# Extra matmuls beside the maxima where two attention units meet, the first unit's turn three items sooner, and GpSimd's padding after the first rows

## The reference

```python
def mla_attention(x, Wq, Wdkv, Wuk, Wuv, Wo, ln_g, ln_b):      # t = 2048 rows, 16 heads of 8
    q = (x @ Wq.T).reshape(b, t, N_HEADS, HEAD_DIM).transpose(0, 2, 1, 3)
    latent = layernorm(x @ Wdkv.T, ln_g, ln_b)
    k = (latent @ Wuk.T) ...; v = (latent @ Wuv.T) ...
    q, k = apply_rope(q), apply_rope(k)
    scores = jnp.einsum('bhqd,bhkd->bhqk', q, k) / np.sqrt(HEAD_DIM)
    scores = jnp.where(causal, scores, -jnp.inf)
    attn = jax.nn.softmax(scores, axis=-1)
    out = jnp.einsum('bhqk,bhkd->bhqd', attn, v)...
    return out @ Wo.T

x = x + mla_attention(rmsnorm(x, norm1_w), ...)
x = x + moe(rmsnorm(x, norm2_w), ...)
```

## Time and profile before

| | |
|---|---|
| three runs, us | 1656.7, 1664.8, 1669.15; median 1664.8 |
| the profiled execution | 1654.05 us, span of the core 1652.3 us |
| mean granted clock of PE | 0.864 |
| busy: PE, DVE, ACT, POOL | 1229.8, 1169.2, 953.3, 582.1 us (74, 71, 58, 35%) |

### The profile page before, as it was taken

One profiled execution on the slowest core, in us unless ns is written; L12 is line 12 of the kernel. 1 busy time (PEld: TensorE's weight loads), 2 busy tenths in 40 slices (PEclk: granted clock), 3 DMA queues, 4 the chain that ended last, 5 costly groups with the idle time before them and its releaser, 6 DMA issues. The chain is left out here.

```text
span 1652.3 us, 36830 instructions
## 1 busy us (share of the span) xinstructions
PE 1229.8 (74%) x14007; PEld 648.0 (39%) x14007; DVE 1169.2 (71%) x2634; ACT 953.3 (58%) x1539; POOL 582.1 (35%) x1039
## 2 busy tenths in 40 slices
PE   2755564466667778999998576776878899998848
PEld 2753454366442222223333265653222222233337
DVE  4348698735768889997775355576888999786235
ACT  2226775322345678888887442244666788878622
POOL 2430078146654331221111564575341111111236
PEclk9977676678569999999999788757999999999869
DMA  9252000021000000000010152000000000000023
GB/s 256 74 175 90 1 4 3 24 67 55 1 3 2 1 2 1 1 2 9 21 28 27 51 138 60 2 1 1 1 2 1 2 1 1 2 1 2 1 76 40
DMA packets 56799, 50.77 MB, mean 31 GB/s; under 512 B 7921, under 2 KB 52066, under 8 KB 56178
## 3 DMA queue, kind: packets, MB, share of 16 engines
q1 hardware_dynamic: 48818, 37.77, 8.2%
q0 software_dynamic: 6864, 9.55, 2.3%
q10 hardware_dynamic: 944, 1.10, 0.2%
HBM read 36.16 MB, written 21.35 MB: 35 GB/s over the span
## 5 line engine op out<-in xcount | busy, mean ns | idle before, releaser
L1902 DVE TENSOR_REDUCE arena<-psum 128x1 f32<-128x512 f32 (+4 forms) x1152 | 681.0, 654 | 141.6 <-PE psum L1708 96.9
L1843 ACT ACTIVATE arena<-psum 128x1024 f32<-128x1024 f32 (+3 forms) x640 | 557.9, 899 | 180.8 <-PE psum L1730 172.0
L1746 PE MATMUL psum<-arena 128*9 128x256 f32 (+2 forms) x4352 | 339.1, 388 | 0.8 <-POOL arena L1962 0.8
L1708 PE MATMUL psum<-arena 64*128 64x128 bf16 (+3 forms) x1664 | 224.9, 319 | 96.4 <-DVE arena L1902 86.1
L1730 PE MATMUL psum<-arena 64*128 64x512 bf16 (+3 forms) x1280 | 228.8, 357 | 22.8 <-ACT arena L1843 15.5
L1962 POOL TENSOR_SCALAR_AFFINE_SELECT arena<-arena 128x256 f32<-128x256 f32 x256 | 103.0, 406 | 369.0 <-ACT arena L1843 365.6
L1708 PEld LDWEIGHTS psum<-arena 64*128 64x128 bf16 x1664 | 69.9, 96 | 274.2 <-DVE arena L1902 233.4
L1730 PEld LDWEIGHTS psum<-arena 64*128 64x128 bf16 x1280 | 63.3, 94 | 175.6 <-ACT arena L1843 77.1
L1746 PEld LDWEIGHTS psum<-arena 128*9 128x9 f32 x4352 | 67.8, 89 | 152.5 <-issue 118.2
L1940 POOL CAST arena<-arena 128x16 bf16<-128x16 f32 x64 | 16.3, 255 | 284.3 <-DVE arena L1907 282.1
L698 ACT ACTIVATE small<-psum,YT 128x128 f32<-128x128 f32 x168 | 52.5, 364 | 93.4 <-PE psum L651 93.2
(11 more groups left out here) (368 smaller groups left out, 2015.1 us busy)
## 6 DMA issues: line engine op xcount, KB each, us to landing
regions<-sorted_rows SPq DMA_DIRECT2D x11, 741.8 KB, 14.1
big_w<-in_w SPq DMA_DIRECT2D x2, 2048.0 KB, 20.3
arena<-taps SPq DMA_DIRECT2D x16, 256.0 KB, 3.4
arena<-taps SPq DMA_DIRECT2D x4, 1024.0 KB, 10.8
ACCn<-regions SPq DMA_DIRECT2D x48, 64.5 KB, 1.8
ACCn<-made_rows SPq DMA_DIRECT2D x12, 256.0 KB, 3.8
w<-in_w SPq DMA_DIRECT2D x2, 1024.0 KB
sorted_rows<-arena SPq DMA_DIRECT2D x1, 1483.5 KB, 14.5
```

Source lines behind the costliest of these rows:

```text
L1708: mm = pe.matmul(psum[:, bank_of(("max", (v, m + r))), at:at + w], plain_q[v % 2][rows, a, i * P:(i + 1) * P], keys[rows, 2 * hq + a, key: ...
L1746: mm = pe.matmul(psum[32 * hh:32 * hh + 9, O_BANK, lo:hi], values[:, tile_of(v, j), 4 * hq + hh, :], prob[(t + hh // 2) % N_PROB][:, hh % ...
L1843: act.activation(prob[t % N_PROB][:, :, off:GW], both, ACT.Exp, scale=INV_SQRT_HD).then_inc(a_got, 1)
L1902: dve.tensor_reduce(place, rows, AX.X, ALU.max).then_inc(a_max_got, 1)
```

## The change

It has six edits. (1) `plan` starts the second pass of unit 0 six items after its last item and not nine. (2) The event "out" moves ahead, to just before an even place, so that it stands ahead of a pair of items, or a little more ahead than before. (3) `thin_pairs` collects the items that stand between the last `weigh` of one unit and the first of the next, and those ahead of the first `weigh` of all; ahead of each such pair PE issues one `keep_warm` matmul, after `bank_free` and into the pair's own bank. By the list these are 52 pairs in each block: the 6 of unit 0, the 6 of unit 1, the first 2 of unit 2, and then 38 at meetings (5, 3, 4, 3, 3, 3, 3, 3 in units 2 to 9, and 2, 3, 2, 3, 0, 1 in units 10 to 15). (4) `turn_out` asks for its bank first, issues two `keep_warm` matmuls and then waits for ACT's `a_took`. (5) GpSimd splits the second tile of query group 2 after unit 0's `chain_shift` and not before it. (6) GpSimd's padding waits until DVE has scaled the first group of rows.

```diff
--- before.py
+++ after.py
@@ -1294,7 +1294,7 @@
         def plan(far):
 
             places = []
-            start = [ITEMS_TO[v + 1] + LEAD for v in range(UNITS)] + [N_ITEMS + LEAD + 4 * TILES_OF[-1]]
+            start = [ITEMS_TO[v + 1] + (LEAD if v else 6) for v in range(UNITS)] + [N_ITEMS + LEAD + 4 * TILES_OF[-1]]
             half_at = [start[v] + (start[v + 1] - start[v]) * s / (2 * TILES_OF[v]) for v in range(UNITS) for s in range(2 * TILES_OF[v])]
             half_at += [half_at[-1] + 2 * k for k in range(1, 24)]
             for v in range(UNITS):
@@ -1310,7 +1310,7 @@
                 places += [(half_at[2 * (TILES_TO[v] + j) + a] + 1.4, "cut", (v, j, a)) for j in range(GT) for a in range(2)]
                 places += [(half_at[2 * (TILES_TO[v] + GT) - 1] + 1.5, "aside", v)]
                 after = half_at[2 * TILES_TO[v + 1]:]
-                places += [(after[2] - 0.2, "take", v), (after[4] - 0.2, "out", v)]
+                places += [(after[2] - 0.2, "take", v), (max(int(after[4] - 0.2) // 2 * 2 - 0.01, after[3] - 0.2), "out", v)]
                 if v in LAST.values():
                     steps = (6, 10, 14) if ORDER[v][0] >= 2 else (6, 8, 9)
                     places += [(after[k] - 0.2, name, ORDER[v][0]) for k, name in zip(steps, ("rows", "project", "square"))]
@@ -1318,7 +1318,7 @@
                     places += [(after[16 + k] + 0.2, name, 0) for k, name in enumerate(
                         ("mean", "root", "norm", "", "", "", "", "logits", "", "", "place")) if name]
                     places += [(after[20 + k] + 0.2, "turn", 2 + k) for k in range(2)]
-            places += [(0.2, "query", 2), (0.3, "aside", -1), (ITEMS_TO[3] + 24.2, "query", 3)]
+            places += [(0.2, "query", 2), (0.3, "aside", -1), (ITEMS_TO[1] + 0.5, "aside", -2), (ITEMS_TO[3] + 24.2, "query", 3)]
             if far:
                 places += [(ITEMS_TO[5] + 4.3 + 3 * a, "power", a) for a in range(64)]
                 places += [(ITEMS_TO[10] + 6.2 + 8 * b, "states", b) for b in range(4)]
@@ -1598,6 +1598,8 @@
                         here, there = slice(SLOT * r, SLOT * r + SLOT), slice(SLOT - SLOT * r, 2 * SLOT - SLOT * r)
                         own_pool(pool.tensor_copy(causal[1][here, :], causal[0][there, :]))
                         own_pool(pool.tensor_copy(pick[1][here, :], identb[there, :]))
+
+                pool.wait_ge(l_rows, NT * B + GT)
                 for part in split_k:
                     own_pool(pool.memset(part[:, :, 48:64], 0.0))
                     pool.memset(part[:, :, 48:51], 1.0)
@@ -1675,6 +1677,18 @@
                     if B or least > 0:
                         pe.wait_ge(a_got, act_base + least)
 
+                def thin_pairs():
+
+                    thin, found = True, set()
+                    for kind, x in events:
+                        if kind == "weigh":
+                            thin = x[1] == TILES_OF[x[0]] - 1 and x[2] == 1
+                        elif kind == "max" and thin:
+                            found.add(x)
+                    return found
+
+                thin = thin_pairs()
+
                 def bank_free(event):
                     if B or number[event] >= 3:
                         pe.wait_ge(a_max_got, dve_base + number[event] - 2)
@@ -1701,6 +1715,8 @@
                     if m == 0:
                         pe.wait_ge(a_got, act_base + number["plain", v] + 1)
                     bank_free(("max", (v, m + 1)))
+                    if (v, m) in thin:
+                        keep_warm(bank_of(("max", (v, m))), 1)
                     at = 0
                     for i, a, key, w in pieces:
                         for r in range(2):
@@ -1750,8 +1766,9 @@
                             mm.then_inc(a_weighed, 1)
 
                 def turn_out(event):
+                    bank_free(event)
+                    keep_warm(bank_of(event), 2)
                     pe.wait_ge(a_took, units + event[1] + 1)
-                    bank_free(event)
                     for i in range(GT):
                         mm = pe.transpose(psum[:, bank_of(event), i * P:(i + 1) * P], ot[:, i * P:(i + 1) * P], ident[:])
                     mm.then_inc(a_max_put, 1)
@@ -1963,7 +1980,7 @@
                                        channel_multiplier=-1).then_inc(a_cut, 1)
 
 
-                tiles_beside = {-1: (2, (0, 1)), 0: (2, (2,)), 1: (2, (3,)), 3: (3, (0, 1)), 4: (3, (2, 3))}
+                tiles_beside = {-1: (2, (0,)), -2: (2, (1,)), 0: (2, (2,)), 1: (2, (3,)), 3: (3, (0, 1)), 4: (3, (2, 3))}
                 own_pool(pool.tensor_copy(number_in(ACCn), token_number.unsqueeze(2)))
                 if far:
                     pool.wait_ge(pair_made, 2)
```

## The result

The changed kernel takes 1688.86 us (median of four runs, 1682.73 to 1699.67), the kernel before 1665.09 (1656.70 to 1669.15) in the same set: a ratio of 1.0156, 95% interval 1.0091 to 1.0221. It is slower by 1.6%, and outside the predicted range (1650 to 1685). Its profiled execution took 1682.73 us, 28.7 more than that of before.

A forecast was written before the change was run, and what follows sets the result against it. DVE's reduces were taken to bound the large units, a pair having 0.03 us to spare, with PE busier in late units. Terms 13 - 5.4 + 1 + 5.6 - 9 - 2.5 - 1 + 0.5 = +2.2 us gave 1667, range 1650 to 1685.

The forecast's parts named there:

- the price of a keep_warm ahead of a pair: Between bank wait and pair: 0.21 us at full clock, 0.42 at half, delaying the reduces behind; 0.2 taken.
- 13 and 5.6: Cost in us of keep_warms ahead of 76 pairs at meetings (+13) and 28 at the stages' starts (+5.6).
- The clock at the start: Start of both attending stages: clock rises about 3 us in, 38 us of half clock become full, -9 us.
- rival (a): The clock doesn't rise at the stages' start, keep_warms cost 0.42 us each there: sum +20, 1685 us; chance 0.10.
- The half clock's worth: Half clock costs 0.24 of its length, between 0.28 from masked pairs and 0.20 behind an output.
- turn_out's keep_warms: Two in turn_out run while PE waits for ACT's copy and the bank; thin cover in late units, +1 us.
- -9 and -2.5: Gains in us from half clock turned full: at the two stages' starts (-9) and in stretches between (-2.5).
- The output ahead of a pair: At 18 meetings, DVE's division is done while PE fills the next pair: 0.3 us gained each, -5.4 us.
- Unit 0 sooner, the tile behind the shift, the padding: Earlier scores fill holes in unit 1, -1 us; the memsets' slowing moves to later row groups, +0.5 us.
- (b): Keep_warms ahead of pairs are free, so 13 and 5.6 fall away: -16 us, 1648; chance 0.08.
- (c): All half clock time comes back at half its length: -25.6 us, in all -12, so 1653; chance 0.07.
- (d): Nothing that can be seen: edits do what they say, all terms near their small ends, 1665 us; chance 0.10.

The follow-up runs named there:

- experiment 10: The changed kernel with keep_warms ahead of pairs kept only at the 76 pairs at meetings of units: 1679.08 us, ratio 1.0080 to the kernel before.
- 5: The changed kernel with each keep_warm ahead of a pair on 64 rows of the array in place of 128: 1673.54 us, ratio 1.0042 to the kernel before.
- 1: The changed kernel without the 104 keep_warms ahead of pairs, those in turn_out kept: 1651.18 us, ratio 0.9940 to the kernel before.
- 9: The changed kernel with keep_warms ahead of pairs kept only at the 28 before the first weighing: 1659.77 us, ratio 0.9988 to the kernel before.
- Experiment 4: The changed kernel with each pair's keep_warm behind the pair, in the next score's or transposes' bank: 1659.62 us, ratio 0.9979 to the kernel before.
- experiment 6: The kernel before with only the output step moved ahead of a pair: 1654.80 us, ratio 0.9933.
- experiment 12: The changed kernel without keep_warms ahead of pairs and with the padding where it was before: 1647.16 us, ratio 0.9901 to the kernel before.
- 2: The changed kernel with no added keep_warm at all, neither ahead of pairs nor in turn_out: 1657.65 us, ratio 0.9972 to the kernel before.
- 11: The kernel before with only two keep_warms added in turn_out ahead of the wait for ACT's copy: 1662.93 us, ratio 0.9986.
- 7: The kernel before with only unit 0's second pass three items sooner and GpSimd's second tile behind the shift: 1664.19 us, ratio 0.9985.
- 8: The kernel before with only the padding moved behind the first group of rows: 1663.68 us, ratio 0.9981.
- 3: The kernel before with only the keep_warms ahead of the thin pairs added: 1691.61 us, ratio 1.0175.

## Why the prediction was wrong, point by point

**The step that failed: the price of a keep_warm ahead of a pair, and its cover.** The prediction took 0.21 us from trains of keep_warms, where one follows its like. Ahead of a pair of 64-row items the distance is 0.32 at full clock and 0.54 at half. I also halved it for the 22 late pairs, since ACT and the scores set the pace about half of the time; experiment 10 gives 0.29 over all 76, so nearly all of them are paid. The mechanism was right, for the matmul does stand on the path from the free bank to DVE's reduce; the size of the term was not. In numbers: 18.6 us were in the sum for the 104 (13 and 5.6), and 31.2 were paid. That is 12.6 of the 20.9 us between the predicted +2.2 and the measured +23.1 in the stages; 3.5 are the clock's and 4.8 the other edits', below. The profiled execution is the fastest of the changed kernel's four, with 437 us at half clock in the whole program where the others have 462 to 499, so on the median the clock's share is larger. That the price lies in this step is shown by 5 (same place and columns, half the rows: 0.21) and by 1, 9 and 10 (the loss goes with their number).

The added 0.1 us was there to be read in the trace of before, wherever matmuls of one form follow those of another. PE and its weight loads shortly ahead of rows 3:

```profile
719.12 0.39 PE L1708 MATMUL psum<-arena 64*128 64x512 bf16 x2
719.35 0.38 PE L1730 MATMUL psum<-arena 64*128 64x512 bf16 x2
719.66 0.62 PE L1746 MATMUL psum<-arena 128*9 128x256 f32 x8
```

```profile
719.12 0.10 PEld L1708 LDWEIGHTS psum<-arena 64*128 64x128 bf16 x2 [0.52 <-DVE arena L1902]
719.13 0.10 PEld L1730 LDWEIGHTS psum<-arena 64*128 64x128 bf16 x2
719.66 0.12 PEld L1746 LDWEIGHTS psum<-arena 128*9 128x9 f32 x8 [0.42 <-issue]
```

The pair and the score are both of 64 rows: 0.23 us from one to the other, and the score's weights are loaded from 0.01 us after the pair began. The weighing has 128 rows and 9 columns of weights: 0.31 us behind the same 512 columns, and its load begins only with it. At full clock a pair or score of 512 columns has a weighing right behind it 358 times in that trace, always after 0.305 to 0.318 us; a score behind a pair comes after 0.21 to 0.22 us in 203 of 215 cases. Experiment 4 shows the same behind the keep_warm itself: 0.32 us to scores and to weighings, 0.23 to transposes that use the whole array like it. So the price of an inserted matmul depends on whether its successor uses the same rows and columns of the array. Where it doesn't, the successor's load isn't begun ahead and some 0.1 us are added. Whether the 0.10 us of the load are those 0.1 us, or something else has to end first, no run here tells.

The Trainium skill (TensorE: Matmul & The Clock Gate, Part 3, The mechanism) says that PE pulls a weight load ahead of running matmuls when it targets a row group that doesn't conflict, or the background weight buffer. The first half agrees with experiment 5 (0.01 us to the item on the free half). The second half would fit the scores' loads, which begin 0.01 us after a pair that fills both halves of the rows. Behind a keep_warm of 128 rows neither is seen: the pair's load begins only 0.32 us after it.

**The clock at the start,** -9 us. It did rise some 5 us after the first pair, and didn't stay: the stretches of rows 2 at the two starts, 27.31 and 17.07 us, became 17.0 and 13.7, and behind the first start another 17.1 us of half clock came up, before unit 3's output. Up to that output the two blocks together have 47.8 us at half where they had 54.6, and experiment 1, without the 28 keep_warms, has 34.1. In all their runs, 9, with the 28 alone, has 27 us less at half than before and 1, with none, 30. So they gave back nothing that stands out; the 38 us that I took don't exist. This part of rival (a) was right: more than two thirds of the 44 us stayed at half.

**The half clock's worth.** I took 0.24 of its length from two pairs of rows; the line gives 0.334 and the runs of before 0.31. Half of its length, the penalty by the Trainium skill's rule that the prediction weighed (TensorE: Matmul & The Clock Gate, Terms), is too much for this kernel, as argued. Where the clock did come back was not the start: of the twelve kernels and the two given, the eight with turn_out's keep_warms have 37.5 to 71.6 us at half and the six without 75.2 to 102.4. These are single executions, but the clocks of all runs go the same way: the kernels with them have 26 to 54 us less at half than before, the others 8 less to 6 more, with one exception, experiment 6 (26 less without any keep_warm). From 81.9 to 58.0 us in the changed kernel is 23.9 x 0.334 = -8.0, where the sum had -9 and -2.5. The size was near by luck, for the cause was another: the prediction gave turn_out's keep_warms no gain.

**The output ahead of a pair,** -5.4. Right at the meeting (0.29 us for 0.30), not seen in the stages' sum. The last three units of each block lose the 2 us again that the others gain, unless turn_out's keep_warms stand there too: in experiment 12 those three gain 1.9 us in the first block in place of losing 2.3. The line shows nothing of this edit beyond the clock (-0.8 us in 6). The runs of 6 are 10.7 us faster on the mean, 8 of it with the clock; whether the edit does that to the clock was not tested further. (The prediction's 0.57 us of division is 0.49 by the rows, 725.94 to 726.43; no term hangs on it.)

**turn_out's keep_warms,** +1. Covered at the meetings, as forecast, by the wait for ACT's copy and for the bank (12 against 2). The cover comes from the new place of the output: without it, in 11, they cost 8.0 us, 0.25 for each of 32 outputs, and the timeline has 0.29. In return they bring full clock, which the prediction didn't have in this term.

**Unit 0 sooner, the tile behind the shift, the padding:** -1 and +0.5. The shift moved as said, the slow scalings moved by one group as said, and experiments 7 and 8 give no difference of either sign.

**The sum again,** with what was measured, for the attending stages: 31.2 - 8.0 - 0.1 for all else = +23.1. The stretch ahead of the first preparing stage adds 5.6 us to the profiled execution. The edits have no part in it: it takes 401.4 to 403.7 us in seven of the fourteen executions and 406.9 to 408.2 in the other seven, 402.5 in experiment 1 and 407.0 in the changed kernel, whose edits all stand behind it. The longer ones have more time at half clock in it (201.8 us in the changed kernel, 174.2 before), but the clock doesn't explain it all: experiment 12 has 199.4 and takes 403.4. The stretch between the blocks does the same (127 us in most, 136 to 139 in four). So the two profiled executions differ by 28.7 us, and the medians by 23.8, and this is why I read the experiments by their stages.

**The rivals.** None came out as written. (a) gives 1685, near the 1688.86, but by the wrong sum: it has the same 13 us for the meetings, and puts the loss into a doubled price at the start, where experiment 9 found some 8 us of the 36. (b), keep_warms that cost nothing, is refuted by 1 and 3. (c), half of the half clock's length, is too much by 0.334 and 0.31, and (d), nothing that can be seen, by the ratio. The condition for the loss was in rows 3 and 4 (a pair has 0.03 us to spare); what was wrong was to price an instruction by its distance to its like, and to halve that price for the late pairs.

## What to carry to other kernels

An instruction inserted ahead of the one that is waited for costs the distance to that successor, so look for a row where the same kinds follow each other: a matmul over all 128 rows ahead of a pair of 64-row matmuls took 0.32 us here, where trains of it showed 0.21. Filler (matmuls that only keep PE busy, for its clock) belongs where PE already waits for another engine; put ahead of the pairs that DVE waited for, it cost 31 us. In turn_out, with the output in its new place, it cost nothing at the meeting that was followed and came with less time at half clock (53 us on the mean of eight kernels, against 87 of six without). Test an edit that creates such a wait (the output's new place) and one that fills it together and each alone: the filler alone brought clock and paid it away (11, 0.9986), the output alone gained 0.7% (6), both 0.6 and 1.0% (1 and 12), and what the filler adds to the output is clear by the clocks, but not by the ratios, whose intervals overlap.

## What was not expected of the hardware

- Keep_warm (128 rows, 512 columns) to a pair of 64-row matmuls: 0.31 to 0.32 us at full clock (93 times), 0.52 to 0.57 at half (11 times), where keep_warm to keep_warm is 0.21 to 0.23 and 0.43. On 64 rows: 0.01 to the item on the other half, 0.23 to the one on its own.
- The step belongs to the change of form: 512 columns on 64 rows to a 128-row, 9-column weighing is 0.305 to 0.318 us 358 times in the trace of before, and to a matmul of 64 rows 0.21 to 0.22. Weight loads begin some 0.2 us ahead between like forms, even on rows that are in use, and not ahead between unlike ones.
- DVE bounds these stages, and yet each microsecond in which PE's clock is at half goes with 0.334 us of length over a range of 44 to 102 us, with deviations below 1 us in six of seven kernels; 86 executions of the kernel before give 0.31 by themselves.
- 64 matmuls in turn_out, two for each output, go with 37.5 to 71.6 us of half clock in place of 75.2 to 102.4. 104 keep_warms ahead of pairs don't: 92.0 us in experiment 3.
- Stretches that no edit touches take 401.4 to 408.2 us and 126.9 to 139.2 us from one execution to the next, each near one of two values. What sets it was not found; time at half clock explains it in part.
